# A software-pipelined attention block: scores follow their maxima by 24 units in place of 32

## What is computed

```python
hn = _layernorm(x, ln1_g, ln1_b)
q = (hn @ wq + bq).reshape(b, s, NH, D).transpose(0, 2, 1, 3)   # NH = 16 heads, D = 8
...
scores = jnp.einsum('bhqd,bhkd->bhqk', q, k) / jnp.sqrt(jnp.float32(D))
attn = jax.nn.softmax(scores, axis=-1)
o = jnp.einsum('bhqk,bhkd->bhqd', attn, v)
x = x + (o @ wo + bo)
hn2 = _layernorm(x, ln2_g, ln2_b).reshape(-1, h)
idx = jnp.argmax(hn2 @ gate_w + gate_b, axis=-1)                # one of E = 8 experts
moe = relu(hn2 @ w1[idx] + b1[idx]) @ w2[idx] + b2[idx]
return x + moe.reshape(b, s, h)
```

## Time and profile before

| what | value |
|---|---|
| median of 3 runs | 1427.96 us (1420.08 to 1430.06) |
| profiled execution | 1424.17 us, of which span 1422.2 us |
| granted TensorE clock over the span | 0.888 |
| busy PE, DVE, ACT, POOL | 80%, 69%, 48%, 44% |
| first expert layer, first maxima to last exponential | about 312 to 551 us |
| last layer, the same | about 1105 to 1345 us |

### The profile page before, as it was taken

How to read it: one execution, slowest core, us unless ns; L and a number is a source line. 1 busy time by engine, 2 the same in 40 slices (tenths; PEclk the granted TensorE clock), 3 DMA queues, 4 the chain that set the end, 5 groups by cost and what they waited for, 6 DMA issues and landing times. The chain is left out here.

```text
span 1422.2 us, 32904 instructions
## 1 busy us (share of the span) xinstructions
PE 1140.9 (80%) x12906; PEld 620.3 (44%) x12906; DVE 986.8 (69%) x2114; ACT 683.9 (48%) x1412; POOL 631.2 (44%) x838
## 2 busy tenths in 40 slices
PE   6746757769999998853788878978986899999975
PEld 2212322323333334742465665656665233333375
DVE  5699999978888884535846646647421897888453
ACT  3843434324776766521442442343430276676744
POOL 2369979864235312531633543443351633251153
PEclk9879888877999999876888988989987699999988
DMA  5378934031241402244142141141110332140223
GB/s 155 134 277 325 339 131 177 30 89 48 46 105 47 113 2 88 65 106 89 28 96 41 30 107 23 28 106 29 26 41 19 69 83 76 50 131 10 85 57 87
DMA packets 131647, 127.63 MB, mean 90 GB/s; under 512 B 86007, under 2 KB 117559, under 8 KB 126106
## 3 DMA queue, kind: packets, MB, share of 16 engines
q1 hardware_dynamic: 123440, 117.65, 29.6%
q0 software_dynamic: 2496, 5.13, 1.1%
q10 hardware_dynamic: 5558, 2.76, 1.0%
HBM read 104.83 MB, written 37.90 MB: 100 GB/s over the span
## 5 line engine op out<-in xcount | busy, mean ns | idle before, releaser
L1399 DVE TENSOR_REDUCE f_row_min<-f_ps 128x1 f32<-128x512 f32 x512 | 327.4, 681 | 62.9 <-PE f_ps L1719 62.4
L1281 ACT ACTIVATE f_e<-f_ps 128x512 f32<-128x512 f32 x512 | 278.5, 598 | 123.0 <-PE f_ps L1738 117.0
L1719 PE MATMUL f_ps<-f_operands 72*128 72x512 bf16 x512 | 204.8, 411 | 20.5 <-DMA f_operands<-k_scr 15.5
L1738 PE MATMUL f_ps<-f_operands 75*128 75x512 bf16 x512 | 189.5, 380 | 2.6 <-ACT f_e L1281 2.1
L789 PE MATMUL m_ps<-m_shared,sb_ident 128*128 128x512 f32 x256 | 135.2, 677 | 58.2 <-DVE m_shared L629 58.0
L362 POOL TENSOR_TENSOR m_drive<-m_du,m_ring 128x1024 f32<-128x1024 f32 x64 | 149.7, 2351 | 56.2 <-DVE m_ps L621 37.5
L494 ACT ACTIVATE m_ps<-m_delta,m_A 128x511 f32<-128x511 f32 x128 | 83.0, 681 | 131.9 <-DVE m_ps L621 109.0
L2541 DVE TENSOR_REDUCE d_row_min<-d_ps 128x1 f32<-128x384 f32 (+3 forms) x176 | 105.0, 634 | 49.8 <-PE d_ps L2766 48.3
L1749 PE MATMUL f_ps<-f_e,f_v_op 128*32 128x512 f32 x1024 | 136.4, 604 | 2.4 <-ACT f_e L1281 1.4
L1719 PEld LDWEIGHTS f_ps<-f_operands 72*128 72x128 bf16 x512 | 51.2, 100 | 162.3 <-DVE f_row_min L1399 110.9
L789 PEld LDWEIGHTS m_ps<-m_shared,sb_ident 128*128 128x128 f32 x256 | 52.3, 215 | 143.4 <-DVE m_shared L629 87.1
(11 more groups left out here) (297 smaller groups left out, 2168.4 us busy)
## 6 DMA issues: line engine op xcount, KB each, us to landing
m_ring<-bc_scr SPq DMA_DIRECT2D x32, 1024.0 KB, 5.2
f_rows_scr<-blank SPq DMA_DIRECT2D x2, 8707.5 KB, 31.1
f_wall<-f_wall SPq DMA_DIRECT2D x16, 578.0 KB
f_operands<-q_scr SPq DMA_DIRECT2D x32, 288.0 KB
f_operands<-k_scr SPq DMA_DIRECT2D x96, 96.0 KB
d_q_op<-q_scr SPq DMA_DIRECT2D x6, 576.0 KB
d_k_op<-k_scr SPq DMA_DIRECT2D x18, 192.0 KB
f_operands<-f_rows_scr SPq DMA_DIRECT2D x46, 64.5 KB, 1.8
```

Of the source, the lines that this page charges most:

```text
L1281: nc.scalar.activation(e_sb[:, n % 3, hh, :], ps[:, SCORE[(b * UNITS + u) % SCORE_BANKS], :], ACT.Exp, scale=SCALE).then_inc(s["e_out"], 1)
L1399: nc.vector.tensor_reduce(row_min[:, b % 2, u // TPB, u % TPB:u % TPB + 1], ps[:, MAXQ[(b * UNITS + u) % MAX_BANKS], :], AX.X, ALU.max, ne ...
L1719: nc.tensor.matmul(ps[:, MAXQ[n % MAX_BANKS], :], q_op(b, QK)[:, hd, t * P:(t + 1) * P], k_op(b, QK)[:, hd, :], start=True, stop=True).the ...
L1738: nc.tensor.matmul(ps[:, SCORE[n % SCORE_BANKS], :], k_op(b, QKS)[:, hd, t * P:(t + 1) * P], q_op(b, QKS)[:, hd, :], start=True, stop=True ...
```

## The change

The lag goes from 32 to 24. Three of the four places of group turns go to 52, 68 and 100 (86 stays). The places that follow in the round of the batch before, `turn_out`, `attended`, `project_out`, the second norm, `turn_again` and the early row tiles, come two steps earlier on every engine. The places of the maxima's splits and turns, of the next batch's norm and projections, of expert choice and ranks, and every queue's own order stay.

```diff
-LAG = 32
+LAG = 24
...
-AT_TURN_GROUP = (55, 71, 86, 102)
+AT_TURN_GROUP = (52, 68, 86, 100)
...
-                if mu == 42:
+                if mu == 40:
                     side_use("attended", last)
-                if mu == 45:
+                if mu == 43:
                     side_use("output", last)
-                if mu == 60:
+                if mu == 58:
                     side_use("hidden", last)
...
-                        if mu == 43:
+                        if mu == 41:
                             attended(last)
...
-                        if mu == 61:
+                        if mu == 59:
                             turned_again(last)
...
+                        if mu == 44:
+                            attended(last)
+                        if mu == 45:
+                            second_stats(last)
                         if mu == 46:
-                            attended(last)
-                        if mu == 47:
-                            second_stats(last)
-                        if mu == 48:
                             second_moments(last)
                             second_variances(last)
...
-                        if mu == 40 and last == B - 1:
+                        if mu == 38 and last == B - 1:
                             pe.wait_ge(s["e_out"], B * UNITS)
                             pe.wait_ge(s["max_out"], B * UNITS)
                             turn_rows(0)
                             turn_rows(1)
-                        if mu == 42:
+                        if mu == 40:
                             turn_out(last)
-                        if mu == 43 and last == B - 1:
+                        if mu == 41 and last == B - 1:
                             up(0)
-                        if mu == 45:
+                        if mu == 43:
                             project_out(last)
...
-                        if mu == 60:
+                        if mu == 58:
                             turn_again(last)
```

More of the change, by code:

```diff
@@ L1346, in _ @@
                     if 0 <= last < B:
-                        if mu == 41 and last == B - 1:
+                        if mu == 39 and last == B - 1:
                             rows_turned(0)
                             rows_turned(1)
-                        if mu == 43:
+                        if mu == 41:
                             attended(last)
-                        if mu == 44 and last == B - 1:
+                        if mu == 42 and last == B - 1:
                             raised(0)
-                        if mu == 50 and last == B - 1:
+                        if mu == 48 and last == B - 1:
                             rows_turned(2)
@@ L1357, in _ @@
                             raised(2)
-                        if mu == 61:
+                        if mu == 59:
                             turned_again(last)
-                        if mu == 62 and last == B - 1:
+                        if mu == 60 and last == B - 1:
                             rows_turned(3)
@@ L1641, in _ @@
                                 stage(j)
-                        if mu == 49 and last == B - 1:
+                        if mu == 47 and last == B - 1:
                             lowered(0)
                             normed_again(last)
-                        if mu == 51 and last == B - 1:
+                        if mu == 49 and last == B - 1:
                             stage(3)
@@ L1858, in _ @@
                             turn_rows(1)
-                        if mu == 42:
+                        if mu == 40:
                             turn_out(last)
-                        if mu == 43 and last == B - 1:
+                        if mu == 41 and last == B - 1:
                             up(0)
-                        if mu == 45:
+                        if mu == 43:
                             project_out(last)
-                        if mu == 47 and last == B - 1:
+                        if mu == 45 and last == B - 1:
                             turn_rows(2)
@@ L1870, in _ @@
                             down(1)
-                        if mu == 60:
+                        if mu == 58:
                             turn_again(last)
-                        if mu == 61 and last == B - 1:
+                        if mu == 59 and last == B - 1:
                             turn_rows(3)
```

## The result

The changed kernel takes 1448.66 us, the median of 4 runs (1446.87 to 1457.34), against 1426.13 of the kernel before in the same sitting (1420.08 to 1430.06, 4 runs). The ratio is 1.015, its 95% interval 1.011 to 1.019: slower by about 22.5 us, where +16.3 was forecast. Ratios leave out executions more than 1.5% above the fastest of the same kernel, medians and ranges do not. A later sitting, with more runs of the kernel before, gives 1.016 again (experiment 1). The profiled execution took 1446.87 us, 22.7 more than that of before.

The account below looks back on a forecast made before the run. It took PE to bound the combined steps, ACT the scores alone and DVE the maxima alone; +4.0 + 9.0 + 5.0 + 4.8 - 6.5 = +16.3 us on 1428.0 gave 1444.3, range 1429 to 1452.

Parts of the forecast that it names:

- part 4: Steady steps: group turns wait for ACT's copy of the maxima, partly covered by DVE; +4.8 us, from -2 to +10.
- Part 1: Start of each layer: steps 24 to 31 gain score matmuls and a weighted product, partly at half clock; +4.0 us.
- Part 2: Batch 0, step 56: PE waits 4.5 us a layer for quarter 2's shifts, queued behind two groups' loads; +9.0 us.
- rival (b): Quarter 2's shifts are not late at step 56, so no clock is lost: +3.7, 1431.7 us; chance 0.10.
- Part 3: Behind the wait at step 56, PE's clock falls to half: +5.0 us for two layers, from 0 to 6.8.
- Rival (a): The wait at step 56 is there but the clock stays: +11.3, 1439.3 us; chance 0.15.
- Part 5: End of each layer: `turn_out` comes earlier, bounded by row tiles landing; -2.5 and -4.0, sum -6.5 us.
- (c): The end decides, start, shifts and turns cost nothing: -10.8, 1417.2 us, 0.8% faster; chance 0.06.
- (d): Shifts late in every quarter, 0.3 us missing at some 25 quarters: +7 on the forecast, 1451 us; chance 0.09.

Follow-up runs that it names:

- experiment 1: The changed kernel run again with no edit, for the scatter: 1449.01 us, ratio 1.016 against 23 runs of the kernel before.
- Experiment 10: Kernel before at lag 32 and lag 24, batch 1's norm turn and projections five steps sooner, quarter 1's shifts ahead of SP's store wait: 1434.32 and 1440.88 us.
- experiment 4: Changed kernel, with SP issuing the shifts of quarter 2 of batch 0 ahead of all group loads of batch 1: 1437.66 us, ratio 1.012.
- experiment 6: Changed kernel, batch 0's order on SP: one group load, quarter 2's shifts, one load, quarter 3's shifts, the other two loads: 1438.97 us, ratio 1.009.
- experiment 7: Kernel before with lag 24, its old places, and batch 0's group loads spread out between the shifts: 1427.04 us, ratio 1.002.
- experiment 5: Changed kernel, with batch 0's quarter 2 shifts issued by ACT on its own queue, right behind its copy of the maxima: 1444.68 us, ratio 1.016.
- Experiment 2: Kernel before with the lag alone changed to 24, every place as before: 1442.54 us, ratio 1.014.
- experiment 9: Kernel before with a lag of 28: 1431.42 us with the old order of loads and shifts, 1424.95 us with the loads spread out between shifts.
- experiment 3: Changed kernel with the old lag of 32, so only the new places are kept: 1447.24 us, ratio 1.018.

## Why the prediction was right

The forecast, 1444.3 in a range of 1429 to 1452, holds the measured 1448.66, and it is slower by over 1%, as was likeliest. The mechanism held in each part but for the cover by DVE in part 4; the sum was 6 us short in the medians, and 9.3 in the stages of the two layers. By its own steps:

**Part 1, the start** (+4.0): mis-sized, +7.4 (4.04 and 3.32). The count of work was right, the clock was not. I took the rise where it is now, at 334.6, or sooner with a fuller PE. It came at 340.6, and in the last layer at 1142.7 in place of 1129.9. With that rise the same count gives 1.7 + 0.85 + 2.6 + 3.3 + 1.3 + 1.1 = 10.85 us, and 10.80 were measured. From 332.7 to 340.6 PE was never idle, 7.90 of 7.90 us, and the clock stayed at 0.50. The +1.5 of the last layer, with a fuller PE raising the clock sooner, was the wrong half of the term. Experiment 10 shows how much is the clock's: 6.33 us for steps 24 to 31 at a clock of 0.97, 8.27 at 0.65.

**Part 2, the shifts of quarter 2** (+9.0): the right transfer, the right step, in both layers, and no other quarter. The stage grew by 12.1 us, which includes what I had put inside it, the wait of the turn at place 52 (0.98 us in the first layer). The last layer's 4.6 is the 4.5 forecast; the first layer's 7.4 has the stores' late landing on top (4.45 us against 2.39), which I had no term for and which came back in every such profile. The landing itself was read rightly: I had it at about 360.1 in the kernel before, and the packets there end at 359.49. The reason was half right: experiments 4, 6 and 7 take the wait away or shorten it to 1.0 and 1.5 us by the order of the loads, but experiment 5 leaves 3.3 us of it on an empty queue. It is the bytes in flight that count, which the drain rate of the earlier trace rows measures in either case. That batches 1 and 2 cost nothing held in this kernel to 0.2 us, with no room to spare: experiment 6 had 1.8 us there. The Trainium skill's fit in "DMA: Bandwidth & Descriptors", section "Anatomy of one DMA — SWDGE (gpsimd) path", which rival (b) weighed, gives 2.0 us for these 12 KB (it is made from DMAs that GpSimd issues, these come from SP and ACT); here they took 7.0, 6.3 and 6.7, and 3.7 with one load ahead. In experiment 10, with the loads through before, they took 2.4 us (issued at 361.30, score at 363.71), which is near the fit.

**Part 3, the clock behind the wait** (+5.0): shown, 4.0 in this profile. The stretches at half clock behind the waits were 6.8 and 3.4 us long here and 10.2 in the repeat, so 5.0 is a mean of something that scatters. Rival (a), a wait without it, fell in every profile with a wait of 1.4 us or more at step 56; the 1.02 us of experiment 6 left the clock alone.

**Part 4, the turns of groups** (+4.8): mis-sized, +9.2. The waits were sized well, 6.1 us in the first layer against 6.8 (0.98 and 0.48 each against 1.05 and 0.6), and `project_out`'s went, 1.2 against 1.7. The step that failed is "DVE catches up while PE stands; I take 2.7 of the rest as covered": DVE's row is 1.5 us against 1.6, so nothing was covered, and 6.1 - 1.2 = 4.9 is the 4.5 measured. Experiment 2 parts it: with the old places the shorter lag alone costs 1.6 and 2.1 us here, as `project_out` waits 2.6 us in place of 1.2, and the places cost 2.7 on top.

**Part 5, the end** (-6.5): -7.0. The sum is right, its parts less so, and that is luck: I had -2.5 and -4.0, and it was -3.5 in both layers. The scores alone gave 4.13 us a layer where I had counted 5.4, and the rows' landing took back 0.68 and 0.60 ahead of `turn_out`. The new bound that I named is there: the turn of a row tile waited 0.63 us for its DMA in the first layer and 0.77 in the last, right before `turn_out`. Experiment 7 shows that the end is all that a shorter lag gives (3.9 and 3.8 us), and that the start uses it up (3.9 and 3.2).

**Rivals.** (b), shifts not late, and (c), the end decides, fell with the wait at step 56. For (b) I wrote that the landing isn't shown; the packets of the trace before show it, 5.5 us after the issue. (c) is what experiment 7 built, with the shifts in time and the old places, and it gave a ratio of 1.002, not 0.992: its part 1 at nothing was wrong, and so was the full 5.4 gained twice. (d), late shifts in every quarter, showed in one quarter, by 0.2 us.

## What to carry to other kernels

When a loop's lag shrinks, list every transfer that the lag covered, add up the bytes that the DMA engines still have to move at its issue, and set the landing against the new need; another queue didn't get it past those bytes here. Where a small transfer has a deadline, put the large loads behind it one at a time, not in a block, and look one transfer further for the next one that the block makes late. Price an idle stretch of PE by the clock behind it as well, and don't book slack on another engine as cover unless that engine's wait is in the waits of before.

## What the runs showed that I had not expected

**The clock didn't rise under a busy PE.** From 332.7 to 340.6 PE was busy 7.90 of 7.90 us at a clock of 0.50, in experiment 9 17.04 of 17.10 (and in the earlier trace rows 7.35 of 7.35). In all three the work was mostly bf16 matmuls over 72 and 75 rows (the earlier trace rows has a mean clock of 0.53). The two stretches around the rise in the changed kernel are these, columns as above:

```profile
337.20:340.60 3.40, 3.40 (x7) 1.11 (x6) 1.38 (x2) 1.42 (x4) 0.00 (x0) 0.50 0.00 0
340.60:344.00 3.40, 3.40 (x19) 1.15 (x18) 1.85 (x3) 2.14 (x5) 0.00 (x0) 1.00 0.00 0
```

The first of them is the one that holds a projection in fp32 over 128 rows (337.41). But the clock rose at 374.72 as well, behind 3.4 us of maxima, scores and eight weighted matmuls, with no projection. Whether rows, type or something else matters was not tried apart.

**The clock fell behind short waits**: for 17.1 and 3.4 us behind 2.04 and 1.71 us (experiment 9), for 10.2 us behind 2.14 (experiment 4), for 3.4 us behind 1.78 and 1.46 (experiments 6 and 7), and behind 1.17 us with smaller gaps around it (experiment 3). A wait of 1.68 us (experiment 4), one of 1.02 (experiment 6) and turns that waited up to 1.25 us in the changed kernel left it alone. So neither the fall nor its length follows from the length of the wait alone.

**An empty queue didn't help a small transfer** while another queue's loads were in flight: 6.7 us from issue to landing, and 3.9 us to its first packet, where it is 1.4 with no loads about (experiment 5).

**Small casts on DVE held by POOL**: 0.82, 0.96 and 1.98 us in place of 0.17 (experiment 10).
